# Softmax attention of a two-layer block: orders and lags of each engine, logits in groups of four, a drain written out

## The chip, the cores and the metric

The kernel runs on one core of a Trainium2 chip. The metric is the device time of one execution in microseconds. A core has five engines that run in parallel, each in its own program order: TensorE (PE in the profile), VectorE (DVE), ScalarE (ACT), GpSimd (POOL), and the queue of SyncE (SP), which here issues the DMAs. They meet only in semaphores: an instruction that waits holds all that stands behind it on its engine.

## The reference

Two layers over x of (8, 512, 256). Each layer modulates, attends, and then sends tokens through experts. The change touches layer 1's attention and the router logits behind it:

```python
Q = (x @ Wq.T).reshape(b, s, h, hd)          # 16 heads of 16
K = (x @ Wk.T).reshape(b, s, h, hd)
V = (x @ Wv.T).reshape(b, s, h, hd)
scores = jnp.einsum('bshd,bstd->bsht', Q, K) / math.sqrt(hd)
attn = jax.nn.softmax(scores, axis=-1)       # over the heads of one token
out = jnp.einsum('bsht,bstd->bshd', attn, V).reshape(b, s, dm)
...
x = x + ga * (out @ Wfc.T)
h = _layernorm(x) * (1 + cb) + sb
logits = h.reshape(T, D) @ Wg                # 8 experts
```

A token attends between its own 16 heads, so nothing crosses tokens. After the logits comes a choice over all 4096 tokens, which can start only when the last tile's logits are there.

## The kernel before, in words

The 4096 tokens are 32 tiles (NT) of 128, four tiles (TB) to a batch. Layer 0 ends at about 516 us with its experts; then the second attention runs to 822 us, then the router's search for thresholds, and from 888 us layer 1's experts. All here is between 526 and 822 us.

Each tile t goes through stages, each a small function on one engine. On SP: load_norm (the normed rows), store_v and load_v (the values go through device memory, to come back in another layout), turn_k (four DMAs a batch that move the keys to other partitions), load_x, layer_rows (three DMAs a batch: gate, scale and shift), store_rows. On TensorE: turn_n (transpose), values, queries_keys, scores, weigh, project (once a batch, all four tiles), turn_h, logits. On ScalarE: shift_h, keep_v, keep_qk, compact (from PSUM to a compact tile, in two halves), exps, keep_oT, rstd2, keep_h1T, keep_logits. On GpSimd: mask_other, sub_max, normalize_exp, add_attention. On VectorE: max_scores, sum_exp, turn_exp, gate_attention (once a batch, four products), stats_sum, norm2.

The path of a tile is load_norm, turn_n, shift_h, values and queries_keys, turn_k, scores, compact, mask_other, max_scores, sub_max, exps, sum_exp, normalize_exp, turn_exp, weigh, keep_oT, project, gate_attention, add_attention, stats_sum, rstd2, norm2, turn_h, keep_h1T, logits, keep_logits.

The order is a software pipeline, tile_steps (line 1366): in step s an engine issues for each entry (lag, stage) of its list the stage of tile s - lag. One set of lags (lines 1362 to 1364) holds for all engines, and each engine has one list and, ScalarE and TensorE, a second one for the steps with project (s mod 4 = 2). There are 47 steps; after them a short loop over the last four tiles does turn_h, logits, norm2, stats_sum and the rest. TensorE fills some waits with hold_clock: products of the identity that nobody reads.

Who shares what: scores (b_s) and project (b_y) write the same four PSUM banks, so scores waits for the gate to have read all four products, and project for the compaction. turn_n, turn_h and logits share bank 6. There are two halves of mod3 (layer_rows), three of sc (scores), two of the transposed exponentials, two rows of h1 for tiles before the last four.

The gate and what waits for it:

```python
def gate_attention(t):
    b = t // TB
    if t % TB == TB - 1:
        eng.wait_ge(c_["y"], b + 1)
        eng.wait_ge(s_m3[b % 2], 48 * (b // 2 + 1))   # layer_rows landed
```

Of the kernel before, what the change touches and what calls it, by code (L numbers as in the profile page):

```python
# [30 lines left out]
E = 8  # L31
# [30 lines left out]
def two_layer_kernel(nc, a):  # L62
    ctx = ExitStack()
    with ctx:
# [1276 lines left out]
        h1T = [cw(D) for _ in range(2 + TB)]  # L1341
# [15 lines left out]
        b_lg = [bank[:, D:D + E] for bank in (ps[6], ps[6], ps[4], ps[5], ps[1], ps[2])]  # L1357
# [4 lines left out]
        LAG_N, LAG_V, LAG_VST, LAG_QK, LAG_VLD, LAG_S = 2, 3, 4, 6, 7, 10  # L1362
        LAG_MX, LAG_EX, LAG_ET, LAG_PV, LAG_Y = 11, 12, 13, 14, 15
        LAG_XLD, LAG_ROW, LAG_X, LAG_H = 14, 16, 19, 20

        def tile_steps(stages, project_steps=None):

            for s in range(NT + LAG_Y):
                for lag, stage in project_steps if project_steps and (s - LAG_Y) % TB == TB - 1 else stages:
                    if 0 <= s - lag < NT:  # L1370
                        stage(s - lag)

        def done_by(t, lag, other, steps_ago=0):

            return min(max(t + lag - other - steps_ago + 1, 0), NT)
# [11 lines left out]
        with nc.Block() as block:  # L1387
            @block.sync
            def _(eng):
# [5 lines left out]
                out_t = fin_d[1][0:T, 0:2 * D].rearrange("(t p) (h d) -> t h p d", p=P, h=2)  # L1395

# [27 lines left out]
                def load_x(t):  # L1424
                    b = t // TB
                    if t % TB == 0:
                        eng.wait_ge(s_fin, 16 * (2 + 2 * B + done_by(t, LAG_XLD, LAG_H, 1)))
# [10 lines left out]
                def store_rows(t):  # L1438
# [3 lines left out]
                tile_steps([(0, load_norm), (LAG_VST, store_v), (LAG_VLD, load_v), (LAG_XLD, load_x), (LAG_ROW, layer_rows),  # L1442
                            (LAG_H, store_rows), (LAG_QK, turn_k)])
                for t in range(FIRST_LAST - 1, NT):
                    store_rows(t)

            @block.gpsimd
            def _(eng):
# [20 lines left out]
                def add_attention(t):  # L1469
                    b, k = t // TB, t % TB  # L1470
                    eng.wait_ge(c_["ya"], b + 1)
                    eng.wait_ge(s_x1[b % 2], 16 * (b // 2 + 1))
                    eng.tensor_tensor(xr[b % 3][:, k, :], xr[b % 3][:, k, :], yb[:, k, :], ALU.add).then_inc(c_["xa"], 1)
                tile_steps([(LAG_ET, normalize_exp), (LAG_X, add_attention), (LAG_MX, mask_other), (LAG_MX, sub_max)])
                for t in LAST:
                    add_attention(t)

            @block.vector
            def _(eng):
# [27 lines left out]
# [3 lines that stand above are left out]
# [3 lines left out]
                        for k in range(TB):  # L1513
                            last = eng.tensor_tensor(yb[:, k, :], b_y[k], mod3[b % 2][:, 0, :], ALU.mult)
                        last.then_inc(c_["ya"], 1)
# [7 lines left out]
                def norm2(t):  # L1523
# [3 lines left out]
                    if t < FIRST_LAST:  # L1527
# [4 lines left out]
                tile_steps([(LAG_H, norm2), (LAG_ET, turn_exp), (LAG_X, stats_sum), (LAG_MX, max_scores), (LAG_EX, sum_exp),  # L1532
                            (LAG_Y, gate_attention)])
                norm2(FIRST_LAST - 1)
                stats_sum(FIRST_LAST)
# [393 lines left out]
```

## Time and profile before

| | us |
|---|---|
| median of 3 runs | 1048.62 (1046.36 to 1049.32) |
| span of the profiled execution | 1045.7 |
| first turn_n of the second attention | 526.2 |
| scores of tile 8, 24, 28 | 607.2, 725.2, 755.1 |
| last project begins | 805.6 |
| first reduction behind the logits | 822.4 |

The span is what lies between the first and the last instruction of one profiled execution. The median of the runs lies 2.9 us above it. Over the whole span PE is busy 92%, DVE 66%, ACT 48%, POOL 36%; these are averages over stages with different limits. Each stage shows its own limit in the busy times of a stretch (a table by windows), in the instructions in order of time, and in what ended an engine's idle time (in brackets behind an instruction, with the idle time). The granted TensorE clock is given as a share of full speed.

### The profile page before, as it was taken

What the parts mean: (1) busy time and instruction counts of PE and PEld (TensorE: products, weight loads), DVE (VectorE), ACT (ScalarE), POOL (GpSimd) and SP (SyncE); (2) the same over time, 40 slices, a digit from 0 to 9 for tenths busy, and PEclk for the clock granted to TensorE, in tenths of its full rate; (3) what the DMA queues carried; (4) which work ended last, traced back from release to release, by engine and by line L of the source; (5) the groups of instructions that cost most, each with busy time, mean ns of one, the idle gap of its engine ahead of it and who ended that gap; (6) DMA issues with size and microseconds to landing.
All of it is one profiled execution on the core that took longest, in us unless ns stands there. A gap on an engine that the chain in (4) does not pass through costs nothing. (4 is left out here: it accounts for less than half of the span.)

```text
span 1045.7 us, 30362 instructions
## 1 busy us (share of the span) xinstructions
PE 959.2 (92%) x11177; PEld 823.6 (79%) x11178; DVE 690.6 (66%) x1747; ACT 496.8 (48%) x1343; POOL 377.1 (36%) x330
## 2 busy tenths in 40 slices
PE   6899999889999999999987999999767888999996
PEld 3466666879999999999965778888666878899995
DVE  3478877855777777777412688889985776344442
ACT  3556665404454554554446777777552440322221
POOL 0134335521223223222213455555561101455552
PEclk9999999999999999999998899999868999999998
DMA  9885581294232222221055657766421620444441
GB/s 338 216 331 122 126 269 41 97 386 115 85 102 79 87 97 85 89 92 71 8 107 92 115 124 150 154 134 128 99 68 57 266 108 22 151 134 140 134 136 35
DMA packets 133025, 135.59 MB, mean 130 GB/s; under 512 B 73884, under 2 KB 122142, under 8 KB 130740
## 3 DMA queue, kind: packets, MB, share of 16 engines
q1 hardware_dynamic: 121684, 90.80, 31.5%
q0 software_dynamic: 11232, 43.27, 13.0%
q8 instruction: 76, 1.25, 0.5%
q14 instruction: 33, 0.27, 0.1%
HBM read 96.21 MB, written 44.77 MB: 135 GB/s over the span
## 5 line engine op out<-in xcount | busy, mean ns | idle before, releaser
L1151 PE MATMUL psall<-rows 128*128 128x128 f32 x1872 | 224.8, 277 | 1.6 <-issue 1.1
L1151 PEld LDWEIGHTS psall<-rows 128*128 128x128 f32 x1872 | 219.6, 194 | 3.1 <-issue 1.3
L1114 POOL DMA_INDIRECT x<-ffn_rows,tok_i x78 | 82.6, 1059 | 171.8 <-DVE tok_i L999 69.9
L1165 PE MATMUL psall<-whi,rows 128*128 x624 | 141.0, 379 | 0.0
L1244 DVE COPY rows<-wlo 128x2048 f32 (+2 forms) x78 | 74.5, 955 | 95.8 <-PE psall L1151 85.2
L1165 PEld LDWEIGHTS psall<-whi,rows 128*128 128x128 f32 x624 | 115.7, 190 | 14.1
L1119 POOL DMA_INDIRECT attn_rows<-rows,tok_i x39 | 41.7, 1070 | 183.9 <-DVE rows L1276 183.9
L1504 DVE STREAM_TRANSPOSE whi<-whi 32x512 f32<-32x512 f32 x128 | 89.7, 701 | 9.1 <-POOL whi L1467 7.7
L1584 ACT ACTIVATE whi<-psall 32x512 f32<-32x512 f32 x128 | 75.3, 588 | 30.8 <-PE psall L1713 27.3
L280 PE MATMUL psall<-cst 128*128 128x128 f32 x714 | 88.4, 280 | 0.5 <-PEq L1387 0.5
L1306 ACT ACTIVATE rows<-psall,vs 128x128 f32<-128x128 f32 x312 | 85.0, 383 | 4.4 <-PE psall L1151 2.1
L280 PEld LDWEIGHTS psall<-cst 128*128 128x128 f32 x714 | 84.1, 195 | 0.8 <-issue 0.6
L1165 PE MATMUL psall<-wlo,rows 128*128 x312 | 73.7, 380 | 0.0
L1457 POOL TENSOR_TENSOR whi<-whi,cst 128x512 f32<-128x512 f32 x32 | 40.7, 1271 | 81.5 <-ACT whi L1584 81.3
L1657 PE MATMUL psall<-wlo,x 128*32 128x128 f32 x2048 | 64.4, 279 | 0.0
L1657 PEld LDWEIGHTS psall<-wlo,x 128*32 128x32 f32 x2048 | 55.5, 112 | 11.3 <-issue 8.6
L1207 ACT ACTIVATE small<-small,eps_t 128x1 f32<-128x1 f32 x39 | 11.6, 297 | 106.4 <-DVE small L1271 106.4
L1165 PEld LDWEIGHTS psall<-wlo,rows 128*128 128x128 f32 x312 | 56.4, 190 | 6.2
L766 PE MATMUL psall<-whi 128*128 128x512 f32 x128 | 58.0, 597 | 1.1 <-ACT key L672 1.1
L1490 DVE TENSOR_REDUCE wlo<-whi 128x16 f32<-128x512 f32 x32 | 21.4, 669 | 54.4 <-POOL whi L1457 54.2
L1744 ACT ACTIVATE rows<-psall 128x256 f32<-128x256 f32 x39 | 15.0, 385 | 84.9 <-PE psall L1139 83.5
L1713 PE MATMUL psall<-whi 16*128 16x128 f32 x1024 | 41.2, 302 | 12.6 <-DMA whi<-whi 4.7
(250 smaller groups left out, 1731.3 us busy)
## 6 DMA issues: line engine op xcount, KB each, us to landing
ffn_rows<-mod_rows SPq DMA_DIRECT2D x2, 4096.0 KB
wlo<-in_W SPq DMA_DIRECT2D x2, 4096.0 KB, 17.5
whi<-in_w SPq DMA_DIRECT2D x5, 1024.0 KB
whi<-mod_rows SPq DMA_DIRECT2D x4, 1024.0 KB, 15.0
ffn_rows<-rows SPq DMA_DIRECT2D x8, 512.0 KB
ffn_rows<-x SPq DMA_DIRECT2D x8, 512.0 KB
wlo<-attn_rows SPq DMA_DIRECT2D x32, 128.0 KB, 3.4
v_turn<-wlo SPq DMA_DIRECT2D x32, 128.0 KB, 2.6
```

The costliest lines, as they stand in the source:

```text
L280: eng.matmul(b_idle, ident, ident, start=True, stop=True)
L766: last = eng.matmul(ps[k % 2][:, :], h0T[:, c, k * P:(k + 1) * P], wqkv[:, c, D:3 * D], start=c == 0, stop=c == C - 1)
L1114: eng.indirect_dma_start(xin[j % DEEP], None, src_d, bass.IndirectOffsetOnAxis(tok_i[:, j:j + 1].bitcast(U32), 0), bounds_check=T, oob_is_ ...
L1119: eng.indirect_dma_start(dst_d, bass.IndirectOffsetOnAxis(tok_i[:, j:j + 1].bitcast(U32), 0), fout[j % 2], None, bounds_check=T - 1, oob_i ...
L1151: last = eng.matmul(b_up[t.par][f // 4][:, (f % 4) * P:(f % 4 + 1) * P], w_now[:, c, f * P:(f + 1) * P], inT[t.par][:, c * P:(c + 1) * P], ...
L1165: last = eng.matmul(b_dn[t.par][:, 0:D], hidT[t.par][:, f * P:(f + 1) * P], w_down[:, bass.ds(e, 1), f, :].rearrange("p o n -> p (o n)"), ...
L1244: eng.tensor_copy(w_now[:, :, part], w_of_e[:, :, part]).then_inc(e_["w"], 1)
L1306: last = eng.activation(dst[:, f * P:(f + 1) * P], banks[f // 4][:, (f % 4) * P:(f % 4 + 1) * P], ACT.Relu, bias=b1T[:, f, bass.ds(e, 1)])
L1504: last = eng.transpose(ebd[t % 2][rows_q, :, 32 * q:32 * q + 32], sc[t % 3][rows_q])
L1584: last = eng.activation(sc[t % 3][rows_q], b_s[rows_q, :, 32 * q:32 * q + 32], ACT.Copy)
L1657: last = eng.matmul(b_qk[t % 2][k * QD:(k + 1) * QD, n * P:(n + 1) * P], wqkv1[:, c, h * QD:(h + 1) * QD], hT[b % 2][:, c, k * P:(k + 1) * ...
L1713: last = eng.matmul(b_s[:, 4 * k + g, :], zqk[b % 2][at, tok, :].rearrange("p t h -> p (t h)"), zk[b % 2][at, tok, :].rearrange("p t h -> ...
```

## The change

What it does:

- Each engine has its own lags and its own two lists (ordinary steps, project steps). The numbers of an engine's steps are no longer common: POOL's mask_other of tile t stands in its step t + 10, while ScalarE's compact stands in its step t + 11.
- The logits of a batch are made at once, turned (experts on partitions, tokens along the row), by group_logits; ScalarE copies four pieces (keep_turned_logits), TensorE transposes them once (turn_logits), ScalarE copies the result (keep_group_logits). Only the last batch keeps logits tile by tile.
- Bank 6 gets one guard, rows_bank_read, which waits for every copy out of it that is outstanding.
- ya is counted per tile, so that add_attention of a tile starts after its own product.
- The loop ends six steps earlier (41 steps); what is left stands written out, call by call, on each engine.
- hold_clock moves: 16 products before project(23), and 62 in the written tail at 15 places.

```diff
-        h1T = [cw(D) for _ in range(2 + TB)]
+        h1T = [cw(D) for _ in range(TB)]
...
+        b_lgT, b_lgB = ps[6][:, D:D + P], ps[6][:, D + P:D + 2 * P]
...
-        LAG_N, LAG_V, LAG_VST, LAG_QK, LAG_VLD, LAG_S = 2, 3, 4, 6, 7, 10
-        LAG_MX, LAG_EX, LAG_ET, LAG_PV, LAG_Y = 11, 12, 13, 14, 15
-        LAG_XLD, LAG_ROW, LAG_X, LAG_H = 14, 16, 19, 20
+        LAG_N, LAG_SHIFT, LAG_V, LAG_KEEP_V, LAG_QK, LAG_KEEP_QK, LAG_Y, LAG_TURN_H = 1, 2, 3, 3, 5, 6, 15, 20
+        LAG_PV, LAG_LG, LAG_TURN_LG, LAG_S, LAG_COMP, LAG_COMP_REST, LAG_EX, LAG_OT = 14, 20, 20, 11, 11, 11, 13, 15
+        LAG_H1T, LAG_KEEP_LG, LAG_KEEP_TURNED, LAG_RSTD, LAG_H, LAG_SUM, LAG_MX, LAG_GATE = 20, 21, 21, 19, 19, 12, 11, 15
+        LAG_STAT, LAG_ET, LAG_MASK, LAG_NORM, LAG_SUB, LAG_X, LAG_NLD, LAG_VST = 18, 12, 10, 11, 11, 17, 0, 4
+        LAG_VLD, LAG_KT, LAG_XLD, LAG_ROW, LAG_ST = 8, 5, 16, 18, 20
+        DRAIN = 6
...
-            for s in range(NT + LAG_Y):
+            for s in range(NT + LAG_Y - DRAIN):
...
-                        eng.wait_ge(s_fin, 16 * (2 + 2 * B + done_by(t, LAG_XLD, LAG_H, 1)))
+                        eng.wait_ge(s_fin, 16 * (2 + 2 * B + len(stored)))
...
-                tile_steps([(0, load_norm), (LAG_VST, store_v), (LAG_VLD, load_v), (LAG_XLD, load_x), (LAG_ROW, layer_rows),
-                            (LAG_H, store_rows), (LAG_QK, turn_k)])
+                tile_steps([(LAG_VST, store_v), (LAG_ST, store_rows), (LAG_ROW, layer_rows), (LAG_NLD, load_norm),
+                            (LAG_VLD, load_v), (LAG_KT, turn_k), (LAG_XLD, load_x)],
+                           [(LAG_VST, store_v), (LAG_ST, store_rows), (LAG_VLD, load_v), (LAG_NLD, load_norm),
+                            (LAG_ROW, layer_rows), (LAG_KT, turn_k), (LAG_XLD, load_x)])
...
-                tile_steps([(LAG_ET, normalize_exp), (LAG_X, add_attention), (LAG_MX, mask_other), (LAG_MX, sub_max)])
+                tile_steps([(LAG_SUB, sub_max), (LAG_X, add_attention), (LAG_MASK, mask_other),
+                            (LAG_NORM, normalize_exp)],
+                           [(LAG_X, add_attention), (LAG_SUB, sub_max), (LAG_MASK, mask_other),
+                            (LAG_NORM, normalize_exp)])
...
-                tile_steps([(LAG_H, norm2), (LAG_ET, turn_exp), (LAG_X, stats_sum), (LAG_MX, max_scores), (LAG_EX, sum_exp),
-                            (LAG_Y, gate_attention)])
+                tile_steps([(LAG_GATE, gate_attention), (LAG_H, norm2), (LAG_SUM, sum_exp), (LAG_MX, max_scores),
+                            (LAG_STAT, stats_sum), (LAG_ET, turn_exp)],
+                           [(LAG_H, norm2), (LAG_GATE, gate_attention), (LAG_SUM, sum_exp), (LAG_STAT, stats_sum),
+                            (LAG_MX, max_scores), (LAG_ET, turn_exp)])
+                sum_exp(29); stats_sum(23); max_scores(30); norm2(22); norm2(23); turn_exp(29); max_scores(31); sum_exp(30)
+                gate_attention(27); sum_exp(31); stats_sum(24); turn_exp(30); stats_sum(25); norm2(24); turn_exp(31)
+                norm2(25); stats_sum(26); stats_sum(27); norm2(26); norm2(27); gate_attention(31); stats_sum(28)
+                stats_sum(29); stats_sum(30); norm2(28); stats_sum(31); norm2(29); norm2(30); norm2(31)
...
+                tile_steps([(LAG_KEEP_LG, keep_turned_logits), (LAG_EX, exps), (LAG_KEEP_TURNED, keep_group_logits),
+                            (LAG_OT, keep_oT), (LAG_KEEP_QK, keep_qk), (LAG_SHIFT, shift_h),
+                            (LAG_COMP, compact_first), (LAG_KEEP_V, keep_v), (LAG_H1T, keep_h1T),
+                            (LAG_COMP_REST, compact_rest), (LAG_RSTD, rstd2)],
+                           [(LAG_EX, exps), (LAG_OT, keep_oT), (LAG_SHIFT, shift_h),
+                            (LAG_KEEP_LG, keep_turned_logits), (LAG_COMP, compact_first),
+                            (LAG_COMP_REST, compact_rest), (LAG_RSTD, rstd2), (LAG_KEEP_V, keep_v),
+                            (LAG_KEEP_QK, keep_qk), (LAG_H1T, keep_h1T), (LAG_KEEP_TURNED, keep_group_logits)])
...
+                def group_logits(t):
+                    if t % TB == TB - 1:
+                        eng.wait_ge(c_["h1T"], t + 1)
+                        rows_bank_read()
+                        put["logits"] += 1
+                        for c in range(C):
+                            for k in range(TB):
+                                last = eng.matmul(b_lgT[QD * k:QD * k + E, :], wg[:, c, :], h1T[k][:, c * P:(c + 1) * P], start=c == 0, stop=c == C - 1)
+                        last.then_inc(c_["lg"], 1)
+
+                def turn_logits(t):
+                    if t % TB == TB - 1:
+                        rows_bank_read()
+                        put["logits"] += 1
+                        eng.transpose(b_lgB, affT, ident).then_inc(c_["lg"], 1)
...
+                tile_steps([(LAG_S, scores), (LAG_V, values), (LAG_TURN_H, turn_h), (LAG_QK, queries_keys),
+                            (LAG_LG, group_logits), (LAG_PV, weigh), (LAG_TURN_LG, turn_logits), (LAG_N, turn_n)],
+                           [(LAG_S, scores), (LAG_V, values), (LAG_TURN_LG, turn_logits), (LAG_QK, queries_keys),
+                            (LAG_Y, hold_last), (LAG_Y, project), (LAG_TURN_H, turn_h), (LAG_PV, weigh), (LAG_N, turn_n),
+                            (LAG_LG, group_logits)])
+                scores(30)
                 hold_clock(eng, 6, b_unread)
-                turn_h(FIRST_LAST - 1)
+                turn_h(21)
                 hold_clock(eng, 3, b_unread)
-                logits(FIRST_LAST - 1)
+                scores(31); weigh(27)
+                hold_clock(eng, 4, b_unread)
+                weigh(28)
                 hold_clock(eng, 12, b_unread)
...
+                project(27); turn_h(22)
+                hold_clock(eng, 4, b_unread)
+                turn_h(23); group_logits(23)
...
+                turn_logits(27)
+                hold_clock(eng, 6, b_unread)
+                turn_h(28); logits(28); turn_h(29)
+                hold_clock(eng, 2, b_unread_late)
+                turn_h(30); logits(29); turn_h(31)
+                hold_clock(eng, 2, b_unread_late)
+                logits(30)
+                hold_clock(eng, 2, b_unread_late)
+                logits(31)
```

## Rows read from the trace of the kernel before

**Rows 1.** Busy time of each engine by stretch, then PEclk, DMA share, GB/s.
```profile
636.90:666.30 29.40, 28.58 (x752) 23.89 (x752) 26.61 (x49) 22.74 (x56) 17.29 (x17) 1.00 0.69 142
...
725.20:755.10 29.90, 23.99 (x664) 20.77 (x664) 27.05 (x49) 18.52 (x42) 17.52 (x17) 0.89 0.55 107
755.10:786.00 30.90, 22.51 (x472) 19.21 (x472) 26.65 (x49) 17.04 (x41) 17.07 (x17) 0.67 0.21 66
786.00:822.30 36.30, 28.99 (x428) 26.95 (x427) 21.98 (x48) 10.32 (x40) 7.43 (x9) 0.91 0.24 78
```

**Rows 2.** Instructions in order of time, TensorE, one steady step and a project.
```profile
647.37 0.44 PE L1677 MATMUL psall<-cst,rows 128*128 128x128 f32 x2
647.74 1.10 PE L1692 MATMUL psall<-whi,wlo 128*32 128x64 f32 x64
648.87 0.61 PE L1701 MATMUL psall<-rows,wlo 128*128 128x8 f32 x4
649.41 1.17 PE L1713 MATMUL psall<-whi 16*128 16x128 f32 x32
...
651.75 1.95 PE L1657 MATMUL psall<-wlo,x 128*32 128x128 f32 x64
653.64 0.44 PE L1677 MATMUL psall<-cst,rows 128*128 128x128 f32 x2
...
660.01 3.74 PE L1668 MATMUL psall<-rows,whi 32*128 32x256 f32 x64
```

**Rows 3.** Groups of ScalarE by line in 636.9 to 666.3 us: busy, mean ns.
```profile
L1584 ACT ACTIVATE whi<-psall 32x512 f32<-32x512 f32 x16 | 9.4, 588 | 2.3 <-PE psall L1713 2.1
L1563 ACT ACTIVATE wlo<-psall,modT 128x128 f32<-128x128 f32 x8 | 3.2, 455 | 0.1
L1591 ACT ACTIVATE whi<-whi 128x512 f32<-128x512 f32 x4 | 2.5, 635 | 0.0
L1576 ACT ACTIVATE whi<-psall 128x512 f32<-128x512 f32 x4 | 2.4, 594 | 0.0
```

**Rows 4.** Groups of VectorE in the same stretch; last, one norm2 of the drain.
```profile
L1504 DVE STREAM_TRANSPOSE whi<-whi 32x512 f32<-32x512 f32 x16 | 11.2, 701 | 0.2
L1531 DVE SCALAR_TENSOR_TENSOR rows<-rows,small,wlo 128x256 f32<-128x256 f32 x4 | 4.3, 1074 | 0.1
L1530 DVE SCALAR_TENSOR_TENSOR rows<-wlo,small 128x256 f32<-128x256 f32 x5 | 2.8, 557 | 0.0
...
L1490 DVE TENSOR_REDUCE wlo<-whi 128x16 f32<-128x512 f32 x4 | 2.6, 662 | 2.1 <-POOL whi L1457 2.1
...
L1514 DVE TENSOR_TENSOR whi<-psall,wlo 128x256 f32<-128x256 f32 x4 | 1.4, 402 | 0.0
...
800.43 0.48 DVE L1531 SCALAR_TENSOR_TENSOR rows<-rows,small,wlo 128x256 f32<-128x256 f32 x1
```

**Rows 5.** SP's issues in order of time: load_norm, turn_k, load_x, load_norm, layer_rows.
```profile
579.42 4.13 SPq L1399 DMA_DIRECT2D wlo<-attn_rows  x1
...
655.71 2.86 SPq L1422 DMA_DIRECT2D whi<-whi  x4
...
661.02 1.90 SPq L1428 DMA_DIRECT2D wlo<-attn_rows  x1
...
668.39 0.45 SPq L1399 DMA_DIRECT2D wlo<-attn_rows  x1
...
670.72 2.07 SPq L1435 DMA_DIRECT2D wlo<-mod_rows  x3
```

**Rows 6.** Landing of layer_rows' DMAs (line 1435), 560 to 800 us.
```profile
DMA to landing us min/median/max: 2.8/3.6/4.6
```

**Rows 7.** Scores of tiles 0 and 4 in order of time, with the wait.
```profile
552.99 2.09 PE L1713 MATMUL psall<-whi 16*128 16x128 f32 x32 [4.75 <-DMA whi<-whi]
...
577.75 2.09 PE L1713 MATMUL psall<-whi 16*128 16x128 f32 x32 [1.34 <-issue]
```

**Rows 8.** Twelve unread products of the drain in order of time.
```profile
801.25 2.84 PE L280 MATMUL psall<-cst 128*128 128x128 f32 x24
```

## What the change was expected to do, before it ran

> **What bounds the kernel now.** I read the second attention batch by batch: the busy time of each engine between the scores of tiles 8, 12, 16, 24 and 28 and the end [rows 1]. Three regimes are to be seen. From 553 to 607.2 us the pipeline fills. From tile 8 to tile 24 (607.2 to 725.2 us, 118.0 us) it is steady, four batches of 29.4 to 29.7 us; in the one shown TensorE is busy 28.58 of 29.40, VectorE 26.61, ScalarE 22.74: TensorE sets the pace. From 755.1 on it drains: 67.2 us in which TensorE does 51.5 and VectorE 48.6 us of work at a granted clock that falls to 0.67, so neither is the bound; waits in the written order are.
>
> Next the order of time in one steady step on TensorE [rows 2]: turn_h at 647.37 and again at 653.64, 6.27 us with nothing idle. The parts, start to start: turn_h 0.37, weigh 1.13, logits 0.54, then scores, turn_n, values and queries_keys 4.23. A project takes 3.74 more. Four steps and one project are 28.8 us; the other 0.6 is the scores that wait for VectorE's gate. Last, VectorE's groups in that batch [rows 4]: its only long wait, 2.1 us a batch, is for the mask behind project.
>
> **Fill, 526 to tile 8.** Queries_keys go out one step earlier against the scores (lag 5, scores lag 11 at the start of their step, which is where lag 10 at the end was). The first scores waited 4.75 us for the DMA of turn_k, and those of tile 4 waited again and then ran at half the clock, 2.09 us where 1.17 is the rule [rows 2, 7]. The first query product can start one turn_n and one values, some 1.8 us, earlier, but turn_k's four issues (2.9 us) and the landing that ended that wait still stand before scores(0), with a load_norm now behind them: 0.7 us gained there. For tiles 0 to 4 before took 24.8 us (552.99 to 577.75). After, ScalarE's order (compaction, values, compaction next to each other, the rest beside the scores) lets a step cost what ScalarE has to do: 2.35 + 0.8 + 0.63 + 0.6 a tile for compaction, shift, exps and keep_qk [rows 3] and, estimated, 0.4 for keep_v, which has half of keep_qk's columns: 4.8 us, 4.9 with a gap: 19.6, a gain of 5.1. For tiles 4 to 8 before took 29.4; after three steps of 5.4 (the steady step without turn_h and logits [rows 2]) and one with project and gate, 9.9: 26.1, a gain of 3.3. Sum 9.1; I take 8.5, with 5 to 9.5 as ends (half of the late DMAs stay; all go).
>
> **Steady batches.** Logits leave: 4 x 0.54 = 2.2 us. In their place once a batch: 8 products onto 8 rows of each quarter. Queries_keys do 64 instructions on 128 columns in 1.95 us [rows 2], so 16 such cost 0.5, and 0.3 to start; a transpose 0.2. But between them stands a new wait: turn_logits waits for ScalarE's four copies, and turn_n, which shares the bank, for the fifth. ScalarE can begin them only when its step is done, so I lay them end to end: copies 1.1 us after the group's products, with weigh (1.13) as cover, then exps 0.65 ahead of the last copy: turn_n 1.0 us late. Queued behind it are the next scores. Project finds its compaction done (4.1 us after the step's start against 3.5). That gives 9.6 (project step) + 7.55 + 2 x 5.7 = 28.55 us, against 29.5: 0.95 gained. ScalarE's 5.7 us step just fits; VectorE, with the mask now ready in time, needs 27.3 of it (29.4 less its 2.1 of waiting), so it doesn't bind.
>
> Against it stands the SP queue. layer_rows moves from lag 16 to 18, the very step in which VectorE's gate reads it. On SP it stands behind turn_k (2.86 us from its first issue), which waits for keep_qk, now one step after its own on ScalarE; behind load_x (1.90); behind two store_v, two store_rows pairs, two load_norm and two load_v (ten issues of 0.45 [rows 5], 5.0 with gaps). keep_qk, which follows the copy of weigh's result, ends about 0.75 us into the 5.7 us step ahead of the project step, 4.95 before that begins, so the third of its three issues (2.07) starts 6.2 us into the step and lands, 3.6 later [rows 5, 6], at 9.9. Project ends at 7.85. The gate waits 2.1 us, the scores behind it 1.75 (0.35 is slack). The trace of before shows no such wait; bounds: 0 (issues as short as the shortest, landing 2.8) and 3.0. So 28.55 + 1.75 = 30.3 for three batches and 29.4 for the fourth, where load_norm has run out: 120.3 against 118.0, a loss of 2.3 (ends: gain of 3.8, loss of 7).
>
> **Tiles 24 to 28.** Before 29.9 [rows 1]. TensorE has little left and VectorE's 27.05 busy us are the bound: 27.0, a gain of 2.9 (1 to 4).
>
> **The drain.** VectorE's 48.6 us of work after scores(28) are the floor, less what runs free of GpSimd: the second instruction of norm2 takes 1.07 us on average in the steady batch and 0.48 alone [rows 4]. I followed the written order with these durations. What VectorE has between scores(28) and the end of turn_exp(31): in the steady batch 26.61 less the gate's 1.4 is 6.3 us a tile, of which the turns are 2.8 (11.2 for four) and norm2 1.63, so 1.87 is sum, max and statistics [rows 4]. Six turns 16.8; six such rests, one max short, 10.6; five norms (20 to 24) free of GpSimd 5.0; gate(27) 1.4; 0.4 of gaps a tile 2.4: 36.2 us. Each operand is there in time: scores(30) and (31) can go 9.6 and 13.4 us in, when ScalarE has emptied the banks; the mask, subtraction and exponential of tile 31 are done by 26.8, where VectorE asks for them at 27.5; project(27) ends by 25.9 and gate(27) starts at 26.1. So VectorE has no gap, since norm2, stats_sum and gate(27) fill what were waits; TensorE idles there, which doesn't matter as long as the clock holds. Then weigh(31) 1.1, its copy 0.4, project 3.74 at full clock: gate(31) at 41.6; its four products and the adds, statistics and norms of the last four, overlapped on VectorE, 7.5; turn_h, copy, logits, key 1.7: 50.8. The products no one reads: 24 instructions, twelve products, take 2.84 us [rows 8], 0.24 each. Those before project(27), weigh(29 to 31) stand in idle time. The ten and more behind turn_h(26) do not: turn_h(31) and logits(31) come 2.1 us later for them. Sum 52.9 against 67.2: 14.3, taken as 14 (8 to 17; project and weigh at 0.67 of the clock cost 3 of that, contention the rest).
>
> **Sum.** -8.5 + 2.3 - 2.9 - 14 = -23.1. What follows the attention is the same instructions, moved as a block. The profiled span of 1045.7 us ends so at 1022.6; the median of the runs shown, 1048.6, lies 2.9 above that span, so 1025.5.
>
> **A rule against it.** The mean of L1531 is 1.07 us in the steady batch against 0.48 in the drain [rows 4]. The Trainium skill, SBUF — State Buffer, Who interferes with whom, says that a VectorE instruction with two SBUF inputs and a GpSimd instruction that reads SBUF exclude each other for their whole length. By that, the trace agrees that order decides the price. It bears on the third rival.
>
> **Rivals.** (a) The layer rows come in time: DMAs land after 2.8 and no issue is held. The steady part then gains 3.8 instead of losing 2.3: 1019.4. For it: the shortest landing; against: the 17.1 us that lie, waits included, between turn_k's first issue and the end of layer_rows' last [rows 5]. Chance 0.22. (b) Slower than before, by one mechanism: SP's issues are held by full rings. One load_norm took 4.13 us to issue where 0.45 is the rule [rows 5]. Two such in the chain from turn_k to layer_rows at each of five gates put 7.2 us more on each: 36 us, 1061. It decides from 23.1/5 = 4.6 us a gate. For it: DMA share is 0.6 to 0.7 [rows 1]; against: the issues in the shown chain run at their normal length in most batches. Chance 0.07. (c) The drain yields less: each of the last 12 norm2 meets a GpSimd operation (0.6 each, 7 us) and the clock drops for one project: 1033. Chance 0.2. (d) The steady step is no longer free of gaps, since ScalarE and TensorE both need 5.7 us and any slip adds: 1 us on each of 20 steps eats all of the gain but 3: 1045.5, about what can't be told from no change. Chance 0.05. The forecast itself keeps 0.46.
>
> **Range.** 1025.5, likely between 1019 and 1033; ends of all terms together give 1013 and 1041. I give 1013 to 1041. About 0.3% (3 us) is what a measurement can tell from no change. Faster 0.88, same 0.04, slower 0.08.
>
> **What would show it.** Fill: scores(8) about 72 us after the first turn_n, no wait of scores(0) above 2 us. Steady: VectorE's L1490 waits gone; a gate whose wait is ended by the DMA of mod_rows, some 2 us each; if none is there, (a). turn_n waiting 0.5 to 1 us for ScalarE once a batch. Drain: from scores(28) to the first reduction of the last stage 53 us, VectorE with under 6 us idle until gate(31). Wrong would be the forecast if a steady batch took over 31 us, or if turn_exp and not the last projection set the drain's end.

## The result, and the profile after

The changed kernel takes 1064.0 us (median; 1061.2 to 1066.2), the kernel before 1048.3: a ratio of 1.016, with an interval of 1.0134 to 1.0186. It is slower by 15.7 us, where 23 us less were forecast. The profiled execution has a span of 1060.5 us against 1045.7.

First the second attention by stretches, cut at the same places as [rows 1]: the scores of tiles 8, 12, 16, 20, 24, 28, and the first reduction of the stage behind. The columns are stretch, length, busy time of PE, PEld, DVE, ACT and POOL with their instructions, then PEclk, DMA share, GB/s.

```profile
602.43:638.20 35.77, 29.64 (x735) 24.52 (x735) 25.27 (x49) 22.08 (x51) 15.99 (x17) 0.88 0.53 114
638.20:675.31 37.11, 32.37 (x753) 26.93 (x754) 25.34 (x49) 23.83 (x57) 15.96 (x17) 0.85 0.54 113
675.31:712.15 36.84, 28.83 (x753) 24.11 (x754) 25.36 (x49) 23.77 (x57) 16.00 (x17) 0.93 0.54 115
712.15:747.76 35.61, 28.83 (x749) 24.51 (x750) 25.36 (x49) 22.36 (x53) 16.00 (x17) 0.88 0.51 103
747.76:780.55 32.79, 28.54 (x633) 25.22 (x634) 24.78 (x49) 18.80 (x43) 15.97 (x17) 0.78 0.50 95
780.55:837.00 56.45, 50.51 (x923) 43.88 (x924) 46.23 (x98) 28.97 (x84) 24.83 (x27) 0.85 0.28 91
```

The fill and the drain gained, though less than forecast. The steady part lost it all and more. Scores(8) come at 602.4 instead of 607.2 us (-4.8). Tiles 8 to 24 take 145.3 us instead of 118.0 (+27.3). Tiles 24 to 28 take 32.8 instead of 29.9 (+2.9). From scores(28) to the reduction at 836.7 it is 56.2 instead of 67.2 (-11.0). That is +14.4 in sum, against 14.8 in the spans. In a steady batch TensorE is now idle 5 to 8 us of 36 where [rows 1] has 0.8 of 29.4, and the granted clock is 0.85 to 0.93 where it was 1.00.

Who waits is in the view of waits of the whole execution (engine and line, what ended the wait: us in total, times, longest):

```profile
POOL wlo L1479 <- DVE whi L1524: 72.8, 8, 11.4
DVE whi L1524 <- DMA wlo<-mod_rows: 39.9, 6, 8.6
PE psall L1760 <- DVE whi L1524: 25.8, 6, 5.8
ACT wlo L1579 <- DMA v_turn<-wlo: 8.6, 5, 3.3
```

VectorE's gate (L1524) waits six times for the DMA of the layer rows, and behind it TensorE's scores (L1760) wait for the gate, 25.8 us in all. The kernel before had no wait of the gate for a DMA, and its scores waited only 3.9 us in all for the gate (5 times, 1.3 at most). One such place in order of time, the project (L1699) of the batch that ends with tile 7, the gate, and scores(12):

```profile
628.15 3.72 PE L1699 MATMUL psall<-rows,whi 32*128 32x256 f32 x59 [0.63 <-issue]
...
636.63 1.42 DVE L1524 TENSOR_TENSOR whi<-psall,wlo 128x256 f32<-128x256 f32 x4 [7.82 <-DMA wlo<-mod_rows]
638.20 2.09 PE L1760 MATMUL psall<-whi 16*128 16x128 f32 x32 [4.56 <-DVE whi L1524]
```

The project ends at 631.9 and the gate starts 4.8 us later. Over six gates these distances are 5.2, 4.8, 2.9, 5.6, 5.6 and 1.8: 26 us. After 4.56 us of idle the scores run in 2.09 us instead of 1.17, which is TensorE's lower clock, 1.2 GHz. Four of the six scores behind gates do so. The other two, behind 2.73 and 1.95 us, run in 1.17, but behind the first of them the value products take 1.95 us instead of 1.13.

And why the rows are late, in SP's issues in order of time ahead of that gate. L1424 is turn_k, L1431 load_x, L1405 store_v, L1443 and L1444 store_rows, L1401 load_norm, L1415 load_v, L1438 layer_rows:

```profile
616.79 2.86 SPq L1424 DMA_DIRECT2D whi<-whi  x4
619.69 1.16 SPq L1431 DMA_DIRECT2D wlo<-attn_rows  x1
620.90 0.83 SPq L1405 DMA_DIRECT2D v_turn<-wlo  x1
621.77 0.43 SPq L1443 DMA_DIRECT2D ffn_rows<-rows  x1
622.25 0.45 SPq L1444 DMA_DIRECT2D ffn_rows<-wlo  x1
622.74 0.50 SPq L1401 DMA_DIRECT2D wlo<-attn_rows  x1
623.33 0.50 SPq L1415 DMA_DIRECT2D wlo<-v_turn  x1
623.88 4.21 SPq L1405 DMA_DIRECT2D v_turn<-wlo  x1
...
629.16 0.40 SPq L1415 DMA_DIRECT2D wlo<-v_turn  x1
629.60 2.78 SPq L1401 DMA_DIRECT2D wlo<-attn_rows  x1
632.42 1.39 SPq L1438 DMA_DIRECT2D wlo<-mod_rows  x3
```

Two issues of 0.45 us are held at this gate, 4.21 and 2.78 us, each right behind a load_v. At the other five the longest single issue is 2.39, 3.61, 4.72, 2.18 and 4.17 us, again next behind a load_v; a second one there takes 1.25, 1.96 and 1.04 us, or is a group of three in 2.04 and 2.07. layer_rows' three issues end 17.0 us after turn_k's first begins (over the six gates 13.4 to 17.0). In the forecast the third of them began 11.15 us after it (4.95 before the project step, then 6.2 into it), so the chain is over 5 us longer. Landing is as it was (median 3.2 us against 3.6 in [rows 6]). So the forecast's chain exists, but with held issues in it, which is rival (b). The runs test that against the other readings: the position in SP's list, the clock, the transfers' size, their pieces.

### The profile page after: what moved, and what is told of

The parts are those of the page before. It is cut to its first block and busy times, and to the rows that moved or that the text cites. A ratio compares the mean times of both kernels' runs of the same rounds, so it can differ in the third digit from the quotient of the medians.

```text
span 1060.5 us, 30500 instructions
## 1 busy us (share of the span) xinstructions
PE 966.9 (91%) x11226; PEld 828.5 (78%) x11227; DVE 679.9 (64%) x1747; ACT 501.1 (47%) x1350; POOL 368.2 (35%) x330
## 3 DMA queue, kind: packets, MB, share of 16 engines
q1 hardware_dynamic: 121684, 90.80, 30.7%
q8 instruction: 76, 1.25, 0.5%
## 5 line engine op out<-in xcount | busy, mean ns | idle before, releaser
L280 PE MATMUL psall<-cst 128*128 128x128 f32 x756 | 99.2, 289 | 0.5 <-PEq L1387 0.5
L280 PEld LDWEIGHTS psall<-cst 128*128 128x128 f32 x756 | 93.7, 202 | 2.0 <-issue 1.5
L1687 PE MATMUL psall<-wlo,x 128*32 128x128 f32 x2048 | 69.1, 291 | 1.8 <-issue 1.6
L1760 PE MATMUL psall<-whi 16*128 16x128 f32 x1024 | 44.4, 318 | 27.7 <-DVE whi L1524 25.8
L1687 PEld LDWEIGHTS psall<-wlo,x 128*32 128x32 f32 x2048 | 59.3, 118 | 12.6 <-issue 11.2
L1760 PEld LDWEIGHTS psall<-whi 16*128 16x128 f32 x1024 | 37.8, 218 | 33.1 <-issue 32.7
```

Of the source, the lines that this page charges most:

```text
L280: eng.matmul(b_idle, ident, ident, start=True, stop=True)
L1687: last = eng.matmul(b_qk[t % 2][k * QD:(k + 1) * QD, n * P:(n + 1) * P], wqkv1[:, c, h * QD:(h + 1) * QD], hT[b % 2][:, c, k * P:(k + 1) * ...
L1760: last = eng.matmul(b_s[:, 4 * k + g, :], zqk[b % 2][at, tok, :].rearrange("p t h -> p (t h)"), zk[b % 2][at, tok, :].rearrange("p t h -> ...
```

## The experiments

Each ran beside the kernel before; in three groups its median was 1046.6 to 1048.8 us.

**LAG_ROW back to 16 in the changed kernel.**

```diff
-        LAG_VLD, LAG_KT, LAG_XLD, LAG_ROW, LAG_ST = 8, 5, 16, 18, 20
+        LAG_VLD, LAG_KT, LAG_XLD, LAG_ROW, LAG_ST = 8, 5, 16, 16, 20
...
-                layer_rows(24); store_rows(21); layer_rows(28); load_x(28); store_rows(22); store_rows(23); store_rows(24)
+                store_rows(21); layer_rows(28); load_x(28); store_rows(22); store_rows(23); store_rows(24)
```

> The changed kernel with one edit on SP: layer_rows at lag 16 instead of 18 (and its call for tile 24 left out of the written tail, since the loop now does it). Theory A, the gate waits for the layer rows: in the changed kernel six gates waited for that DMA, 39.9 us of VectorE's time, and began 26 us in all after their project's end; scores behind five of them ran at half the clock. With the rows issued ahead of turn_k the waits go, a steady batch falls from 36.3 us to 28.5 to 29.5, and the kernel to 1020 to 1030 us. Theory B, the new order is too tight by itself (turn_logits and bank 6 waits, ScalarE's 5.7 us step) and the gate only shows it: the waits for the DMA go, others take their place, steady batches stay over 32 us and the kernel over 1045.

Measured: 1030.9 us (1027.5 to 1032.3), ratio 0.983 (0.980 to 0.987), 33 us less than the changed kernel for one number. Its stretches, same cuts (the last ends at the reduction):

```profile
602.03:630.98 28.95, 27.20 (x735) 22.60 (x735) 24.77 (x49) 21.88 (x51) 16.11 (x17) 1.00 0.59 127
630.98:660.70 29.72, 27.54 (x755) 23.34 (x754) 25.33 (x49) 23.75 (x58) 16.04 (x17) 1.00 0.64 131
660.70:691.50 30.80, 27.90 (x755) 23.47 (x754) 25.73 (x49) 23.75 (x58) 16.06 (x17) 1.00 0.67 149
...
721.19:749.64 28.45, 25.42 (x633) 22.83 (x634) 24.55 (x49) 19.23 (x45) 15.99 (x17) 0.88 0.60 113
749.64:804.94 55.30, 47.88 (x922) 41.72 (x922) 45.74 (x97) 29.07 (x85) 24.84 (x27) 0.90 0.28 92
```

The gate no longer waits for a DMA but only for project (19.0 us in all, 7 times), and starts as soon as that is done:

```profile
596.67 3.73 PE L1699 MATMUL psall<-rows,whi 32*128 32x256 f32 x64
600.47 1.42 DVE L1524 TENSOR_TENSOR whi<-psall,wlo 128x256 f32<-128x256 f32 x4 [4.53 <-PE psall L1699]
...
602.03 1.17 PE L1760 MATMUL psall<-whi 16*128 16x128 f32 x32 [0.23 <-DVE whi L1524]
```

Steady batches are back to 119.2 us in sum at clock 1.00. So the late rows explain the whole of the loss, the half clock included. The time lies 0.9 us above Theory A's range and a batch 0.3 above its 29.5, but far from Theory B's. (The expectation counts five scores at half the clock in the changed kernel; there are four.) The rest of the change gains 15.7 us against the kernel before in its own group of runs (17.4 against the 1048.3 above).

**LAG_ROW stays 18, but layer_rows goes first in SP's project step.**

```diff
-                           [(LAG_VST, store_v), (LAG_ST, store_rows), (LAG_VLD, load_v), (LAG_NLD, load_norm),
-                            (LAG_ROW, layer_rows), (LAG_KT, turn_k), (LAG_XLD, load_x)])
+                           [(LAG_ROW, layer_rows), (LAG_VST, store_v), (LAG_ST, store_rows), (LAG_VLD, load_v), (LAG_NLD, load_norm),
+                            (LAG_KT, turn_k), (LAG_XLD, load_x)])
```

> The changed kernel with layer_rows still at lag 18, but first in SP's list of a project step instead of behind store_v, store_rows, load_v and load_norm. In the changed kernel these took from 628.1 to 632.4 us in the batch I read, 2.8 of it one held load_norm. Theory A: the gate's lateness of 1.8 to 5.6 us falls by about 4 each, to 0 to 1.5; kernel 1028 to 1040. Theory B: little moves, over 1050.

Measured: 1035.2 us (1028.1 to 1038.3), ratio 0.986 (0.981 to 0.992). The gate still waits for the rows (19.0 us in 5 waits), but only 5.2 us in 4 waits reach the scores. SP's issues in one batch:

```profile
645.44 2.87 SPq L1424 DMA_DIRECT2D whi<-whi  x4
...
651.99 0.41 SPq L1415 DMA_DIRECT2D wlo<-v_turn  x1
652.44 4.62 SPq L1438 DMA_DIRECT2D wlo<-mod_rows  x3
657.10 0.43 SPq L1405 DMA_DIRECT2D v_turn<-wlo  x1
```

The store_v that was held now issues in 0.43 us, and the three row loads, which have taken its place behind load_v, need 4.62 instead of 1.39. The hold falls on whatever stands behind the load. The rows' issues end 11.6 us after turn_k's first begins, and 29 us come back: it is the place in the queue that counts, not the lag as such.

**The one lag alone, in the kernel before.**

```diff
-        LAG_XLD, LAG_ROW, LAG_X, LAG_H = 14, 16, 19, 20
+        LAG_XLD, LAG_ROW, LAG_X, LAG_H = 14, 18, 19, 20
```

> The kernel before with one edit: layer_rows at lag 18 instead of 16, all else as it was. Theory A, with SP's queue as the place: there too the rows come behind turn_k and load_x, in the step of the gate; each of eight gates waits some us, and the kernel takes 5 to 30 us more than before (1053 to 1078). If the order of before leaves SP so early that the rows still land in time, it stays within 2 us of before, and the lateness is a thing of the new SP order, not of the lag alone.

Measured: 1077.3 us (1076.6 to 1078.2), ratio 1.028 (1.025 to 1.031): +30.7 us. The same wait and the same half clock appear in the old order:

```profile
DVE whi L1514 <- DMA wlo<-mod_rows: 21.9, 6, 4.7
```

```profile
647.06 2.09 PE L1713 MATMUL psall<-whi 16*128 16x128 f32 x32 [5.27 <-DVE whi L1514]
```

The cost of the lag is about the same in both orders (30.7 and 33.1 us), so the lag alone is enough. That the two numbers are so close is in part chance, for the rows are late in different ways. Here their issues end only 8.5 to 10.0 us after turn_k's first begins, with no hold above 2.6 us among them, but turn_k itself begins only 7.5 to 8.1 us before the project's end (at five gates of six). In the changed kernel it begins 12.3 to 15.4 us before it, and the held issues use that up.

**Unread products while the gate is waited for.** In the project step, 20 products on a bank that queries_keys has left stand behind turn_n.

```diff
+                def hold_gate(t):
+                    eng.wait_ge(c_["qke"], min(t + 10, NT))
+                    hold_clock(eng, 20, ps[4][:, 0:P])
...
                             (LAG_Y, hold_last), (LAG_Y, project), (LAG_TURN_H, turn_h), (LAG_PV, weigh), (LAG_N, turn_n),
+                            (LAG_Y, hold_gate),
```

> The changed kernel with its late layer rows, plus 20 unread products (4.8 us at full clock) on TensorE behind turn_n in each project step, where it waits for the gate. It tells the wait from what the clock adds: a steady batch lost some 7.5 us against my sum, of which the gate's lateness beyond the forecast is 3 and half-clock scores, values and queries behind it 2 to 3. If the clock is that part, it stays at 1.0 over the gate, and the kernel falls by 8 to 15 us to 1049 to 1056. If the clock is not on the path (VectorE and ScalarE set the step behind the gate), it stays at 1062 to 1066, or rises where the products outlast the wait.

Measured: 1057.1 us (1053.7 to 1060.8), ratio 1.009 (1.006 to 1.013), 6.9 us less than the changed kernel, where I had expected 8 to 15; the gate still waits 31.9 us for the rows in 5 places. The scores behind all six gates run in 1.17 us. But the 6.9 us are a net figure: at two gates the products outlast the wait and hold the scores themselves, by some 4.5 and 1.7 us. The first of these places:

```profile
665.78 1.42 DVE L1524 TENSOR_TENSOR whi<-psall,wlo 128x256 f32<-128x256 f32 x4 [5.33 <-PE psall L1699]
...
667.30 4.63 PE L280 MATMUL psall<-cst 128*128 128x128 f32 x40
```

A better measure is the stretch from scores(8) to scores(28), with the delay of the scores behind the project's end at its five gates, both against the kernel with LAG_ROW 16 (147.6 us, delays of 1.6 to 1.7). The changed kernel takes 30.5 us more for 20.2 us more of delay; this run takes 21.6 more for 24.4. So, as an estimate, some 10 of the 33 us are the clock's, at the least the 7 that came back, and the rest is the waiting itself.

**The 512 KB load_x taken out of turn_k's step**, in the changed kernel and in the one with LAG_ROW 16.

```diff
-        LAG_VLD, LAG_KT, LAG_XLD, LAG_ROW, LAG_ST = 8, 5, 16, 18, 20
+        LAG_VLD, LAG_KT, LAG_XLD, LAG_ROW, LAG_ST = 8, 5, 14, 18, 20
```

> The changed kernel with LAG_XLD 16 -> 14 alone: the 512 KB load_x leaves the step in which turn_k issues four DMAs of 128 KB and goes behind layer_rows in the project step. In the trace of after, SyncE's store_v of that step is held 4.21 us and a load_norm 2.78 us, always right behind a load_v, and layer_rows starts about 16 us behind turn_k. Theory A (the issue is held because the transfers of that one step pile up ahead of it: turn_k, load_x, two stores, two loads, 1.6 MB in 5 us): with load_x gone the held issues of that step fall below 1.5 us each, layer_rows starts 3 to 6 us earlier, the gate waits less; 1038 to 1056 us. Theory B (load_v's small pieces alone hold what follows it, whatever else is in flight): the holds of 3 to 4 us stay, the gate waits as before, and load_x behind layer_rows changes nothing; 1060 to 1068 us.

> e1 (the changed kernel with LAG_ROW 16) with LAG_XLD 16 -> 14 as well. In e1 the gate no longer waits for the rows, and what is left of the holds is a store_v held 3.71 to 4.12 us, behind which ScalarE's keep_v waits for its buffer (4.5 us, twice), so that a batch takes 29.2 to 30.8 us instead of the forecast's 28.55. Theory A (pile-up of one step's transfers): the hold shrinks, keep_v comes free, a batch takes 28.5 to 29.5 us, 1025 to 1030 us. Theory B (load_v's pieces): the hold stays, 1029 to 1033 us, equal to e1.

Measured: 1060.6 us (1055.6 to 1062.1), ratio 1.009 (1.006 to 1.013), and 1031.3 (1028.0 to 1033.1), ratio 0.982 (0.979 to 0.985). In the first, SP's issues stand so:

```profile
614.88 2.86 SPq L1424 DMA_DIRECT2D whi<-whi  x4
...
621.41 2.94 SPq L1405 DMA_DIRECT2D v_turn<-wlo  x1
...
625.85 2.40 SPq L1401 DMA_DIRECT2D wlo<-attn_rows  x1
628.29 1.38 SPq L1438 DMA_DIRECT2D wlo<-mod_rows  x3
```

The holds shrink from 7.0 to 5.3 us and the chain from 17.0 to 14.8, but the gate's total wait is what it was (39.1 us) and the time moved by 3.5 us; both times lie in Theory B's ranges, though the holds fell. The edit does two things at once: load_x now stands right behind the rows. Over the six gates the issues of the rows end 1.3 us sooner after turn_k's first (13.7 us on average, 15.0 in the changed kernel), but the gate starts 4.5 us after that end instead of 3.4. So bytes ahead in the queue lengthen the holds a little, and this run cannot say what they alone would cost; in the kernel with the rows in time they cost nothing.

**load_v in whole rows.** The same 128 KB, as 128 rows of 1 KB instead of 2048 pieces of 64 bytes. It leaves out the regrouping of the values by head, so it is a probe and no kernel to use.

```diff
-                    cells = vp[b % 3][:, HD:].rearrange("p (g e) -> p g e", e=VW)
-                    eng.dma_start(cells[:, k * GR:(k + 1) * GR, 0:HD], v_d[t].rearrange("(g t) (h d) -> (t h) g d", g=GR, d=HD)
-                                  ).then_inc(s_vld[b % 2], 16)
+                    at = HD + k * GR * VW
+                    eng.dma_start(vp[b % 3][:, at:at + D], v_d[t]).then_inc(s_vld[b % 2], 16)
```

> The changed kernel (LAG_ROW 18) in which load_v moves the same 128 KB as 128 rows of 1 KB instead of 2048 pieces of 64 bytes. It leaves out the regrouping of the values by head, so the attention weighs other numbers; every other instruction, wait and byte is as in the changed kernel. Theory A (what is queued behind load_v's 2048 pieces in the step of turn_k is held, and by that the layer rows come late): the held store_v and load_norm (4.21 and 2.78 us) fall to 1 us or less, the third layer_rows starts 5 us earlier, the gate waits 0 to 2.5 us instead of 6 to 8, and the time is 1034 to 1048 us. Theory B (the bytes of that step hold it, whatever their pieces): the holds stay at 2.5 to 4.5 us, 1058 to 1066 us.

Measured: 1035.1 us (1028.4 to 1037.0), ratio 0.987 (0.982 to 0.991), 28.9 us less, with LAG_ROW still 18. SP's chain at the same gate, and what follows:

```profile
612.87 2.86 SPq L1423 DMA_DIRECT2D whi<-whi  x4
...
619.45 0.74 SPq L1415 DMA_DIRECT2D wlo<-v_turn  x1
620.24 0.46 SPq L1405 DMA_DIRECT2D v_turn<-wlo  x1
...
621.76 0.40 SPq L1415 DMA_DIRECT2D wlo<-v_turn  x1
622.20 1.07 SPq L1401 DMA_DIRECT2D wlo<-attn_rows  x1
623.32 1.38 SPq L1437 DMA_DIRECT2D wlo<-mod_rows  x3
...
629.16 1.42 DVE L1523 TENSOR_TENSOR whi<-psall,wlo 128x256 f32<-128x256 f32 x4 [4.26 <-DMA wlo<-mod_rows]
630.73 1.17 PE L1759 MATMUL psall<-whi 16*128 16x128 f32 x32 [1.01 <-DVE whi L1523]
```

Both holds are gone, and the rows' issues end 11.8 us after turn_k's first begins instead of 17.0 (over the six gates 11.0 on average instead of 15.0). The six scores behind gates wait 2.2, 1.0, 1.2, 0.7, 1.1 and 1.4 us. From 560 to 780 us the packets fall from 73858 to 24363 for about the same megabytes (24.1 and 26.1), and the DMA share from 0.55 to 0.46. So the holds come from load_v's small pieces. Whether what fills up is a queue's store of descriptors or the engines' own time, no row separates, since both fall together. The Trainium skill, DMA: Bandwidth & Descriptors, Why small descriptors are slow (HBM only), gives a fixed overhead for each packet and each descriptor beside the bytes, for transfers that involve HBM. The packet counts and DMA shares just given agree in direction. That this overhead is what holds the issuing queue, no row shows.

**Four buffers for keep_v's rows**, on top of LAG_ROW 16.

```diff
-        vrow = [cw(D) for _ in range(2)]
+        vrow = [cw(D) for _ in range(4)]
...
-        s_vst = [sem(f"s_vst{i}") for i in range(2)]
+        s_vst = [sem(f"s_vst{i}") for i in range(4)]
...
-                    wait_some(eng, s_vst[t % 2], t // 2, 16)
-                    eng.activation(vrow[t % 2], b_v, ACT.Copy).then_inc(c_["ve"], 1)
+                    wait_some(eng, s_vst[t % 4], t // 4, 16)
+                    eng.activation(vrow[t % 4], b_v, ACT.Copy).then_inc(c_["ve"], 1)
```

> e1 with four buffers for keep_v's rows instead of two (vrow, with a semaphore each), so that ScalarE's keep_v no longer waits for the store_v that is held in SyncE's queue. Theory A (that wait is on the path: 4.5 us in two places, and a little in each batch of 29.5 to 30.8 us against the 28.55 of TensorE's own work): 2 to 5 us less, 1026 to 1029 us. Theory B (ScalarE makes the time up elsewhere, since TensorE waits in those steps for instruction issue and for turned logits instead): 1029 to 1033 us, equal to e1.

Measured: 1028.8 us (1027.3 to 1033.4), ratio 0.984 (0.981 to 0.987), not to be told from 0.983 with two buffers. ScalarE's wait for the store is gone and scores(8) come at 597.5 instead of 602.0, but tiles 8 to 24 take 120.6 us instead of 119.2. The median lies at the edge between the two theories' ranges; the 2.1 us are within the scatter of the runs (1027.3 to 1033.4), so this stays open.

**No unread products in the last six steps**, with LAG_ROW 16: the 62 products of the written out part are left out (two of its fifteen places shown).

```diff
                 scores(30)
-                hold_clock(eng, 6, b_unread)
                 turn_h(21)
-                hold_clock(eng, 3, b_unread)
                 scores(31); weigh(27)
```

> e1 without the 62 unread products of the written out last six steps (hold_last ahead of project(23) stays). In e1 the drain from scores of tile 28 to the end takes 55.3 us, at a granted clock of 0.87 to 0.93 in its windows. Theory A (the unread products fill waits and keep the clock): without them the waits stay as long, and the products behind them run at half clock: some 24 transposes and small products, the project of 3.7 us and the next stage's start, 3 to 10 us more, 1034 to 1041 us. Theory B (they lie on the path as often as they fill it, some 62 by 0.24 us = 15 us of TensorE time, and the waits behind them end before them): 0 to 5 us less, 1026 to 1031 us.

Measured: 1030.5 us (1029.1 to 1032.5), ratio 0.983 (0.980 to 0.985), the same as with them. From scores(28) to the reduction it takes 55.4 us against 55.3. Single scores do slow down without them (2.09 us at 762.87, 1.17 with them), but the last two projects take 3.74 us either way, and these set the end. The products are worth nothing here.

**The last six steps by the lists**, with LAG_ROW 16: every engine runs its step lists to the last tile, the last four tiles' logits go one by one at lag 20, and there are no unread products behind the lists.

```diff
-        DRAIN = 6
+        DRAIN = -6
...
                 def group_logits(t):
-                    if t % TB == TB - 1:
+                    if t >= FIRST_LAST:
+                        logits(t)
+                    elif t % TB == TB - 1:
```

> e1 (the changed kernel with LAG_ROW 16) without the order written out for the last six steps: all engines run the same lists of a step to the last tile, the logits of the last four tiles one by one at their lag, and no unread products in that part. In e1 the drain from scores of tile 28 to the end takes 55.3 us, in the kernel before 67.2. Theory A (the written out order is where the drain's 11.9 us come from): without it 6 to 12 us come back, 1037 to 1043 us. Theory B (they come from the lags and the grouped logits, and the order by hand mostly repeats what the lists give): 0 to 4 us, 1030 to 1035 us.

Measured: 1039.1 us (1035.6 to 1040.4), ratio 0.992 (0.990 to 0.994), 8.2 us more than with the written order. Its drain:

```profile
746.13:809.53 63.40, 40.30 (x798) 32.48 (x798) 46.05 (x97) 29.32 (x84) 24.73 (x27) 0.72 0.28 84
```

```profile
766.08 6.13 PE L1686 MATMUL psall<-rows,whi 32*128 32x256 f32 x64 [3.17 <-ACT whi L1584]
...
788.70 6.68 PE L1686 MATMUL psall<-rows,whi 32*128 32x256 f32 x64 [0.50 <-ACT whi L1597]
```

It takes 63.4 us instead of 55.3, and both projects run at half the clock, 5.3 us in sum above 3.74 each. In the run before this one neither did, also without unread products. So the written order is worth about 8 us of the drain's 12. Up to 5.3 of them are the two projects' clock: ahead of the first TensorE sits idle for 3.17 us, and 3 us ahead of the second for 4.47. The other 4 us come with the lags and the grouped logits, which I did not take apart.

## Why the prediction was wrong, point by point

**The step that failed** is the SP queue's chain ahead of layer_rows, and with it the chance given to rival (b). Its place was right: the gate waits for mod_rows, the scores wait for the gate. Its size was not. "Ten issues of 0.45 [rows 5], 5.0 with gaps" took them at a short row. In the changed kernel one issue at each gate is held for 2.2 to 4.7 us and often a second for 1 to 2.8, and at the gate shown the rows are issued 5 us later for it. I took the load_norm of 4.13 us in [rows 5] for an exception of the fill. It is none: in the trace of the kernel before, between 560 and 800 us, all 15 issues (or groups of three) right behind a load_v take 1.70 to 4.13 us. Even the load_x of 1.90 and the layer_rows of 2.07 in [rows 5] stand behind one. Two more, from the steady part:

```profile
606.99 2.30 SPq L1399 DMA_DIRECT2D wlo<-attn_rows  x1
...
641.59 0.38 SPq L1413 DMA_DIRECT2D wlo<-v_turn  x1
642.01 3.73 SPq L1435 DMA_DIRECT2D wlo<-mod_rows  x3
```

So the argument against rival (b), that the issues "run at their normal length in most batches", was a misreading. The 17.1 us named against rival (a) hold 2.4 us of waits; the 14.7 left were near the chain that came (13.4 to 17.0 us), and the sum had 11.6. Rival (b) was priced at 36 us over the forecast, 1061 us; the holds cost 28.9 us by the run with whole rows, and the time was 1064.0. That these are so close is partly luck, since (b) put 7.2 us on each gate where the chain grew by 2.7 to 5.2, and had nothing for the clock. My lower and upper bound for the steady part (0 and 3.0 us of wait at a gate) came from landings and short issues and left the holds out.

**Without the holds the term came out near its number, in part by luck.** With load_v in whole rows the scores behind gates waited 0.7 to 2.2 us, where 1.75 was forecast; at the gate shown the third row load was issued 11.4 us after turn_k's first, where 11.15 was forecast; tiles 24 to 28 took 27.0 us, as forecast. But two other terms were off and cancelled: there the project ended 15.1 us after turn_k's first issue and not 12.8, and the gate started 4.9 us after the third row's issue and not 3.6. The time was still 1035.1, not 1025.5: a batch took 31.4 us (31.05, 32.21, 31.89, 30.57) instead of 30.1, the drain 56.0 instead of 52.9, and the fill gained 7.5 instead of 8.5.

**The clock at the gates** was not in the sum at all. A longer wait there makes the scores, values and query products behind it slow: by the run with unread products at least 7 us of the 33, and some 10 by the estimate made there.

**Steady batch without a wait:** forecast 28.55, measured 29.8 with LAG_ROW 16 (119.2 for four). Measured start to start between 688.43 and 718.14 in the kernel with four buffers, the steps take 7.36, 5.53, 6.28 and 10.54 us against 7.55, 5.7, 5.7 and 9.6. The step with the project was mis-sized by 0.9 (the gate's 0.23, 0.73 of instruction issue), the one ahead of it by 0.6. Not a gain of 0.95 a batch but a loss of 0.3.

**Fill:** forecast -8.5; measured -4.8, -5.2 with LAG_ROW 16, -7.5 with whole rows, -9.7 with four buffers. Part of that lies ahead of the fill: counted from the first turn_n, scores(8) came after 78.2 us (81.0 before), where about 72 was forecast. The changed kernel's first gate waits for its rows, and with two buffers keep_v waits for the held store_v. Both are the same queue. The two waits of [rows 7] are gone: the scores of tiles 0 and 4 run in 1.17 us.

**Tiles 24 to 28:** forecast 27.0; measured 32.8, and 28.45 with the rows in time.

**Drain:** forecast 52.9; measured 56.2, and 55.3 with LAG_ROW 16. There the last gate starts 42.4 us after scores(28), against 41.6; behind it come 12.9 us instead of 11.3. Rival (c) did not happen: the second instruction of norm2 takes the short time everywhere, in the drain and in a steady batch (here of the changed kernel, 638.20 to 675.31), 0.49 us against 1.07 in [rows 4]. Part of that came back on the first instruction, 0.77 us instead of 0.56:

```profile
L1539 DVE SCALAR_TENSOR_TENSOR rows<-wlo,small 128x256 f32<-128x256 f32 x4 | 3.1, 765 | 2.6 <-ACT small L1564 2.5
L1540 DVE SCALAR_TENSOR_TENSOR rows<-rows,small,wlo 128x256 f32<-128x256 f32 x4 | 1.9, 485 | 0.1
```

**The unread products** were charged 2.1 us; they cost nothing measurable and give nothing.

**What would show it** named the sign: "over 31 us" a batch. It was 36.3. The chance of 0.07 for the one rival that had its mechanism in the trace was too small; a held issue on a queue that a new wait depends on is a reason to look at every issue that stands in the same place.

## What to carry to other kernels

Before a load is moved closer to the wait that needs it, add up what stands ahead of it in its issuing queue with the longest issues that the trace shows, not the usual ones, and look for transfers in small pieces among them. A load that nothing has to precede costs nothing two steps earlier: this one lag was worth 33 us, about twice what the rest of the change gained. A wait that reaches the engine that sets the pace is paid a second time in its clock, here 7 us of the 33 at the least. The same late load can cost the same in two orders for different reasons, so its chain is to be read in each.

## What the runs showed of the hardware

- A single DMA's issue on SP takes 0.44 us in the median (changed kernel, 560 to 800 us). The 14 issues or groups of three that followed a load of 2048 pieces of 64 bytes within half a microsecond took 1.04 to 4.72 us there; a store, a load of another tile or three row loads alike, whichever stood there. Where more than 4 us passed first, the next single issue behind such a load took 0.32. With the same bytes in 1 KB rows ten of 14 took 0.32 to 0.50 us, and the longest was 1.41, a group of three. The longest store_v issue between 560 and 780 us was 1.73 us instead of 4.72.
- TensorE ran at its lower clock right behind idle times of 4.19 to 6.00 us at gates (scores in 2.09 us), and at 2.4 GHz behind 1.01 us (1.17). In between the clock fell while the work behind the wait ran. Behind 2.21 us, scores(8) with whole rows, the 32 products took 1.50 us; behind 3.12 us, scores(8) with load_x at lag 14, they took 1.17, and the value and query products after them 1.47 and 3.23 instead of 1.13 and 1.95.
- The last idle time does not decide alone: in the kernel with LAG_ROW 16 a scores at 736.20 took 2.09 us behind 1.06 us of idle, in a stretch at a mean clock of 0.88.
- Unread products in the waits of the drain changed nothing where the order already kept TensorE at work ahead of the two projects. In the lists' order, without them, both projects ran at the lower clock (6.13 and 6.68 us instead of 3.74).

The best of these kernels is the changed one with LAG_ROW 16, at 1030.9 us with two buffers or 1028.8 with four, 1.6 to 1.7% faster than the kernel before.
